# Delta-rule attention with a triangular solve on VectorE: another layout of the solved matrices, and work moved from VectorE to ScalarE and GpSimd

## The reference

```python
h = layernorm(x)
rk = h per head / its norm;  wk = rk shifted by one time step
v = h @ Wv.T; gate = sigmoid(h @ Wg.T); beta = sigmoid(h @ Wb.T)
for t in time:                       # S: 32x32 state of each batch row and head
    err = (v_t - wk_t S) * beta_t
    S = S + wk_t^T err
    o_t = (rk_t S) * gate_t
x = x + layernorm(o @ Wo.T)
x = x + layernorm(ffn(layernorm(x))) # weights rounded to -1, 0, 1, inputs scaled by a global maximum
```

## Time and profile before

| | |
|---|---|
| median of 3 runs | 2191.5 us (2188.45 to 2197.18) |
| profiled execution, its own time | 2184.31 us |
| its span | 2182.6 us |
| granted TensorE clock, mean | 0.979 |
| PE, DVE, ACT, POOL busy | 94%, 91%, 81%, 79% of the span |
| first phase | to about 1870 us, 128 tiles at 13.5 us a step in its middle |

### The profile page before, as it was taken

One profiled execution on the slowest core, in us unless ns is written; L12 is line 12 of the kernel. 1 busy time (PEld: TensorE's weight loads), 2 busy tenths in 40 slices (PEclk: granted clock), 3 DMA queues, 4 the chain that ended last, 5 costly groups with the idle time before them and its releaser, 6 DMA issues. The chain is left out here.

```text
span 2182.6 us, 124273 instructions
## 1 busy us (share of the span) xinstructions
PE 2061.6 (94%) x50225; PEld 1310.3 (60%) x50225; DVE 1978.3 (91%) x5817; ACT 1761.9 (81%) x3759; POOL 1733.0 (79%) x3098
## 2 busy tenths in 40 slices
PE   5689999999999999999999999999999986699997
PEld 3366666666666666666666666666666653455553
DVE  5888999999999999999999999999999993788886
ACT  6778888888888888888888888888888644577775
POOL 6688999999999999999999999999999854244443
PEclk7799999999999999999999999999999999899999
DMA  4223333333333333333333333333333322688885
GB/s 123 55 67 95 99 102 103 100 99 103 100 104 99 102 103 101 100 103 101 101 100 102 100 102 101 100 102 101 102 101 94 84 79 77 211 223 227 229 230 116
DMA packets 171997, 247.78 MB, mean 114 GB/s; under 512 B 54904, under 2 KB 54912, under 8 KB 171424
## 3 DMA queue, kind: packets, MB, share of 16 engines
q1 hardware_dynamic: 171424, 239.85, 41.0%
HBM read 104.40 MB, written 67.11 MB: 79 GB/s over the span
## 5 line engine op out<-in xcount | busy, mean ns | idle before, releaser
L693 DVE TENSOR_TENSOR ps_elim<-ps_elim,sys 128x30 f32<-128x30 f32 (+14 forms) x1920 | 544.2, 327 | 0.7
L701 DVE TENSOR_TENSOR sys<-sys,ps_elim 128x30 f32<-128x30 f32 (+14 forms) x1920 | 535.8, 317 | 1.0
L905 PE MATMUL ps_v<-wv,xt 128*128 128x512 f16 x1536 | 428.1, 388 | 16.7 <-DMA kbd<-kt 13.2
L905 PE MATMUL ps_y<-wo,ot 128*128 128x512 f16 x1536 | 398.4, 382 | 11.5 <-DVE x L834 10.4
L944 PEld LDWEIGHTS ps_chain<-rhs,t_t 32*32 32x32 f32 x16384 | 256.2, 144 | 111.2 <-issue 104.9
L944 PE MATMUL ps_chain<-rhs,t_t 32*32 32x32 f32 x16384 | 284.5, 217 | 6.6 <-DVE rhs L802 4.7
L576 ACT ACTIVATE state<-ps_s 128x512 f32<-128x512 f32 x128 | 76.5, 598 | 221.1 <-PE ps_s L1008 221.0
L1336 PE MATMUL ps_f<-wq,f_xq 128*128 128x512 f16 x1024 | 243.9, 383 | 6.6 <-DVE f_xq L1302 6.6
L1008 PEld LDWEIGHTS ps_s<-err,key_b 32*32 32x32 f32 x16384 | 167.7, 105 | 110.1 <-issue 109.9
L905 PEld LDWEIGHTS ps_v<-wv,xt 128*128 128x128 f16 x1536 | 120.8, 98 | 150.6 <-issue 79.6
L1184 POOL TENSOR_TENSOR f_y_veps<-f_y_var,y_eps 128x1 f32<-128x1 f32 x128 | 53.6, 419 | 187.1 <-ACT f_unread L1217 187.1
(11 more groups left out here) (185 smaller groups left out, 5051.7 us busy)
## 6 DMA issues: line engine op xcount, KB each, us to landing
x_in<-in_L_attn_x SPq DMA_DIRECT2D x512, 64.0 KB
kbd<-kt SPq DMA_DIRECT2D x512, 64.0 KB, 2.4
key_bd<-key_t SPq DMA_DIRECT2D x512, 64.0 KB
x_res<-in_L_attn_x SPq DMA_DIRECT2D x512, 64.0 KB, 2.3
x_scratch<-x SPq DMA_DIRECT2D x128, 256.0 KB, 2.3
f_x<-x_scratch SPq DMA_DIRECT2D x32, 1024.0 KB, 7.7
out<-f_res SPq DMA_DIRECT2D x128, 256.0 KB, 3.7
gate<-gates SPq DMA_DIRECT2D x128, 7.9 KB
```

The lines of the kernel that those rows point to most:

```text
L693: dve.tensor_tensor(tmp, factors(r, c, first, end)[:, c - first:C - 1 - first, c - first:c - first + 1].to_broadcast(shape), sys[:, r, c:c ...
L701: dve.tensor_tensor(dst, dst, tmp, ALU.add).then_inc(elim_done[r], 1)
L905: last = pe.matmul(out, lhs[:, a, kb, :], weights[:, w, kb, :], start=(i == 0), stop=(i == 3 * KB - 1))
```

## The change

It does five things. The solved matrices get the layout [partition, 2, 2, head, row], row innermost, so L944 reads its weights side by side and L709 writes each element 128 bytes from the one before. The two copies of multipliers go from VectorE to ScalarE: the old one to the head of ScalarE's step, the young one behind L478; where the young pair's first columns are meant (even steps), ScalarE waits for `diag_done`, that is for L649. The squares of x move on ScalarE from behind L515 to behind L569. The guard L825 goes to GpSimd, behind L418. On VectorE the sum of squares and the extremes come before the first third of the eliminations.

```diff
-        t_t = sb("t_t", [P, 2, C, 2, H])
+        t_t = sb("t_t", [P, 2, 2, H, C])
...
+                n, l, live = on(base, j, LAG_TURN)
+                if live:
+                    wait(pool, s["ss_sum"], n + 1)
+                    wait(pool, s["ln_done"], n - 1)
+                    wait(pool, s["rn_half"], n - 1)
+                    pool.tensor_scalar(ss[:, l % 2, :], ss_raw[:, :], NORM2_MIN, None, ALU.max).then_inc(s["ss_done"], 1)
...
         def _(act):
+            def multipliers(base, j, ahead):
+
+                lo, hi = columns(j)
+                if ahead == 1:
+                    lo, hi = lo + HALF - 1, hi + HALF - 1
+                q, live, r, before = pair(base, j, ahead)
+                if live:
+                    if lo == 1:
+                        act.wait_ge(s["diag_done"], q + 1)
+                    else:
+                        act.wait_ge(elim_done[r], before * (C - 2) + (lo - 1))
+                    nc.scalar.activation(factors(r, lo, lo, hi), sys[:, r, lo + 1:C, lo:hi], ACT.Copy).then_inc(elim_mult[r], 1)
+
             def step(base, j):
 
+                multipliers(base, j, 1)
...
                     nc.scalar.activation(rhs[:, :], ps_chain[:, :], ACT.Copy).then_inc(s["turned_done"], 1)
 
+                multipliers(base, j, 2)
...
-                    wait(act, s["ss_sum"], n - 1)
-                    nc.scalar.activation(x_sq[:, l % 2, :], x_in[:, l % 4, :], ACT.Square,
-                                         scale=sc[:, 0:1], bias=sc[:, 1:2]).then_inc(s["sq_done"], 1)
...
                                          ACT.Copy).then_inc(s["kt_done"], 1)
+
+                n, l, live = on(base, j, LAG_XHAT)
+                if live:
+                    wait(act, s["ss_sum"], n - 1)
+                    sc = ln_sc[:, l % 2, :]
+                    nc.scalar.activation(x_sq[:, l % 2, :], x_in[:, l % 4, :], ACT.Square,
+                                         scale=sc[:, 0:1], bias=sc[:, 1:2]).then_inc(s["sq_done"], 1)
...
-            def multipliers(base, j):
-
-                lo, hi = columns(j)
-                for (q, live, r, before), lo, hi in ((pair(base, j, 1), lo + HALF - 1, hi + HALF - 1), (pair(base, j, 2), lo, hi)):
-                    if not live:
-                        continue
-                    if lo == 1:
-                        dve.wait_ge(s["diag_done"], q + 1)
-                    else:
-                        dve.wait_ge(elim_prod[r], before * (C - 2) + (lo - 1))
-                    dve.tensor_copy(factors(r, lo, lo, hi), sys[:, r, lo + 1:C, lo:hi]).then_inc(elim_mult[r], 1)
...
-                    dve.transpose(t_t[:, r, :, :, :].rearrange("p i a h -> p i (a h)"), sys[:, r, :, :]).then_inc(s["tt_done"], 1)
+                    dve.transpose(t_t[:, r, :, :, :].rearrange("p a h i -> p i (a h)"), sys[:, r, :, :]).then_inc(s["tt_done"], 1)
...
                 systems(base, j)
                 diagonal(base, j)
                 if j % 2 == 0:
                     right_side()
-                multipliers(base, j)
-                if j % 2 == 0:
-                    solve(base, j, third(j, 0))
-                else:
-                    solve(base, j, third(j, 0)[:1])
+                squares()
+                extremes()
+                if j % 2 == 1:
                     right_side()
-                    solve(base, j, third(j, 0)[1:])
...
+                solve(base, j, third(j, 0))
...
-                            last = pe.matmul(ps_chain[q, e], t_t[q, l // 2 % 2, :, l % 2, h], rhs[q, e], start=True, stop=True)
+                            last = pe.matmul(ps_chain[q, e], t_t[q, l // 2 % 2, l % 2, h, :], rhs[q, e], start=True, stop=True)
```

More of the change, by code:

```diff
@@ L226, in later, with pair, columns, factors @@
                     ps_xt.rearrange("p (m t) -> p m t", t=C))
+        def pair(base, j, ahead):
+            q = j // 2 + ahead
+            return times(base, BODY // 2, q), base is not None or 0 <= q < NT // 2, q % 2, times(base, BODY // 4, q // 2)
+        def columns(j):
+            return (1, 8) if j % 2 == 0 else (8, HALF)
+        def factors(r, c, lo, hi):
+            return ps_elim[r][:, MULT:MULT + (C - 1 - lo) * (hi - lo)].rearrange("p (i k) -> p i k", k=hi - lo)
         block = ctx.enter_context(nc.Block())
@@ L629, in _ @@
         def _(dve):
-            def pair(base, j, ahead):
-                q = j // 2 + ahead
-                return times(base, BODY // 2, q), base is not None or 0 <= q < NT // 2, q % 2, times(base, BODY // 4, q // 2)
             def systems(base, j):
@@ L802, in right_side, with squares, extremes @@
                         dve.tensor_tensor(rhs[:, :], val[:, l, :], ps_chain[:, :], ALU.subtract).then_inc(s["rhs_done"], 1)
+                def squares():
+                    m, k_l, k_live = on(base, j, LAG_TURN)
+                    if k_live:
+                        wait(dve, s["sq_done"], m + 1)
+                        wait(dve, s["ss_done"], m)
+                        dve.tensor_reduce(ss_raw[:, :], heads(x_sq[:, k_l % 2, :]), AX_X, ALU.add).then_inc(s["ss_sum"], 1)
+                def extremes():
+                    n, l, live = on(base, j, LAG_MAX)
+                    if live:
+                        wait(dve, s["z_done"], n + 1)
+                        dve.wait_ge(s["max_done"], n + 1)
+                        dve.tensor_tensor(k["z_ends"][:, 0, :], ps_zn[:, :], k["z_ends"][:, 0, :], ALU.max).then_inc(s["max_done"], 1)
+                        dve.wait_ge(s["min_done"], n + 1)
+                        dve.tensor_tensor(k["z_ends"][:, 1, :], ps_zn[:, :], k["z_ends"][:, 1, :], ALU.min).then_inc(s["min_done"], 1)
                 systems(base, j)
@@ L807, in step @@
                     right_side()
-                multipliers(base, j)
-                if j % 2 == 0:
-                    solve(base, j, third(j, 0))
-                else:
-                    solve(base, j, third(j, 0)[:1])
-                    right_side()
-                    solve(base, j, third(j, 0)[1:])
[L816 to L825, removed]
+                squares()
+                extremes()
+                if j % 2 == 1:
+                    right_side()
+                solve(base, j, third(j, 0))
                 n, l, live = on(base, j, LAG_RES)
@@ L836, in step @@
                 solve(base, j, third(j, 1))
[L838 to L844, removed]
                 n, l, live = on(base, j, LAG_V)
```

## The result

The changed kernel takes 2315.0 us in the median (2313.1 to 2316.7) against 2190.2, 1.056 times as long (95% interval 1.054 to 1.058). It is slower, as forecast, but by 125 us where 20 were forecast, outside the stated range. The span of the profiled execution is 2311.4 us.

The account below looks back on a forecast made before the run. TensorE was taken to bound the kernel; even 14.35 plus odd 13.06 gave 27.41 us a pair against 27.04, +23 us over 62 pairs, -4 at the end: 2204 us profiled, 2211 median. Whole range 2158 to 2262.

Parts of the forecast that it names:

- TensorE's saving: L944's weight loads reach L1008's pace, each half 0.37 us shorter: 0.74 us a step off TensorE's queue.
- ScalarE's additions: Multiplier copies add 0.14 and 0.24 us in even steps, 0.10 and 0.22 in odd; moved squares fit the hole before L576.
- The even step and its added wait: ScalarE's young copy waits 1.23 us for VectorE's L649, delaying TensorE's L987: the even step lasts 14.35 us.
- The transposed write: L709 on VectorE, writing elements 128 bytes apart: taken as 0 us extra, with +0.65 us kept as a rival.
- rival 1: L709's spaced write costs what the spaced load cost, 40 us more: 2251 us; chance 0.20.
- The odd step: Loop from L576 through ScalarE's L541 and TensorE's L987 to L1008: from 13.52 to 13.06 us.
- The baseline: One even and one odd step from the middle of the first phase, before the change: 27.04 us a pair.
- The last steps: Projections gone and VectorE left, spared 1.3 us a pair over some 3 pairs: -4 us.
- GpSimd: The guard adds 0.21 us a step; its queue needs 26.94 us a pair, still under 27.41.
- the forecast's 19: Whole-kernel sum: +23 us from about 62 pairs at +0.37 us each, less 4 us in the last steps.

Follow-up runs that it names:

- young_late: The changed kernel with the young copy of even steps later on ScalarE, behind the half-precision copy of x (L551): 2190.8 us, 1.001 of the kernel before.
- undo_layout: The changed kernel with the solved matrices back in their old layout, all else as changed: 2247.1 us, 1.028 of the kernel before.
- both_behind_pool: As both_behind, but with the guard on GpSimd as in the change: 2186.7 us, 0.998 of the kernel before.
- young_1: The changed kernel with the young copy of even steps one operation later on ScalarE, behind the variance of y (L522): 2245.0 us, 1.024 of the kernel before.
- young_2: The changed kernel with the young copy of even steps two operations later on ScalarE, behind the variance of x1 (L530): 2202.2 us, 1.005 of the kernel before.
- fill_one: The changed kernel plus one 512-column matmul of zeros on TensorE in even steps, before it waits for the Gram copy: 2348.7 us, 1.072 of the kernel before.
- late_guard_back: As young_late, with the guard moved back to VectorE, behind the sum of squares: 2204.4 us, 1.006 of the kernel before.
- only_layout: The kernel before with the new layout of the solved matrices alone: 2219.8 us, 1.014 of the kernel before.
- both_behind: Changed kernel, old copy behind turned prediction, even-step young copy behind variance of x, VectorE's old even-step order, guard on VectorE before residual: 2174.3 us, 0.992.

## Why the prediction was wrong

- **TensorE's saving.** 144 to 105 ns and a half in 0.68 us, as the prediction took it, at best. From start to next start the halves of L954 last 0.82 us in the mean in young_late, 0.76 without the waits that stand behind some of them, against 1.06 before: about 0.3 of the 0.37 us came.
- **ScalarE's additions.** Right but for a little: the copies of 105, 210, 64 and 184 elements hold the queue 0.19, 0.28, 0.15 and 0.25 us where 0.14, 0.24, 0.10 and 0.22 were taken; the squares did fit behind L569 (now L602).
- **The even step and its added wait.** Right in mechanism and, with the old transpose, in size: 14.46 measured in undo_layout, 14.35 worked out. This step gave the sign. The wait came at the operation and with the releaser that were named.
- **The transposed write: the term that was mis-sized.** The prediction took 0 us, by the row of L649, and kept +0.65 us as rival 1 with a chance of 0.20. It measured +0.78 us (1965 - 1189 ns), 48 us over 62 pairs. A write of 32 elements in 85 ns could not tell: at a pace of 0.83 ns an element only 27 of its 85 ns depend on the pace at all, and a constant's fill reads nothing. The nearer row was the load with the same 128-byte spacing. The rule of the Trainium skill that the prediction quotes (page "Advanced Engine Details and Errata", section "SBUF Cachelines") makes no exception for writes; the trace agrees.
- **TensorE's clock: the step that was missing.** The prediction gave TensorE's hole a length and no consequence. Where it was 1.69 to 2.10 us long the granted clock fell behind it in 18 of 28 cases, and the prediction's 3.90 us from L987 to the state update's end became 5.41 there, 1.4 us more than in the other steps: 15.99 - 15.23 = 0.76 us a pair, 47 us in all. The clock loss came with the longer hole only: without the spaced write (undo_layout) there was none. So the two misses are not independent, and rival 1, which had the write right, still fell short at 2251.
- **The odd step.** 13.06 worked out, 13.32 measured: 0.26 x 62 = 16 us. The loop was the right one: in the mean of the odd steps the second half of L954 takes 0.84 us where the first takes 0.70, since the transposes of x wait 0.15 us for the Gram copy. Its terms were each a little short: from L616 to the end of L574 9.14 us (9.06 taken, the copies' 0.08), from L997 to the end of L1018 3.97 (3.90), the two hand-overs 0.10 each (0.06 and 0.04).
- **The baseline.** I took 27.04 us a pair from one stretch; over 500 to 1500 us the mean is 27.24. That is 12 us the other way.
- **The last steps.** The prediction took 4 us off there. From the state copy of step 120 to that of step 127 the changed kernel loses 5.3 us against the one before; four of these seven steps show a granted clock of 0.79 to 0.87, before it two, at 0.84 and 0.86.
- **GpSimd.** The guard costs 0.35 us of queue, not 0.21 (0.49 us from the start of L432 to that of L445, 0.14 from L418 to L424 before). It was not what ended the steps of the changed kernel; its place on GpSimd costs 12 us in both_behind_pool.

Added up: the forecast's 19, the write 48, the clock 47, the odd step 16, less 12: 118 of the 125 us. The last steps (9) and the even step's 0.1 us (7) would make it 134; the stretch overstates the whole a little, for over the first 120 steps a pair loses 1.99 us, not 2.07. The two large terms, the write and the clock, stand apart from such errors.

## What to carry to other kernels

A copy that is moved to a less busy engine takes its wait along; ask which chain ends in that wait, and put the copy as far down the new queue as its reader allows: here the same instruction cost 125 us or nothing by its place. A hole in TensorE's work is not only its own length: price what the clock may do behind it. And a layout that suits the reader may be paid by the writer, as here; measure both sides before choosing, best with each alone.

## What the runs showed of the hardware

- VectorE's 32x32 transpose of 1024 elements a partition takes 1.19 us writing side by side and 1.97 us writing 128 bytes apart, a factor of 1.65; the weight loads read at the same spacing take 144 against 105 ns.
- Behind waits of 1.69 to 2.10 us on TensorE the granted clock fell in 18 of 28 steps of the changed kernel (to 0.60 over 4.3 us in the step shown), at 1.4 us a step; behind waits of up to 1.59 us (six steps there, all of young_1, young_2 and undo_layout) it was never under 1.00. Where most of such a hole was filled with a product of zeros (fill_one), it fell in 15 of 33.
- A VectorE instruction of 0.17 to 0.20 us, the guard, took 0.84 and 1.13 us when it met a long GpSimd instruction, and in all 74 such cases of three runs (late_guard_back 37, only_layout 22, both_behind 15) it ended 0.03 us after it; VectorE's other instructions beside the same GpSimd work kept their mean length within 0.03 us.
